# Cross-attention kernel: output tiles of batches 11 to 14 copied by ScalarE with the residual added by GpSimd, and query scores ahead of key scores in the late rounds

## The reference

```python
text = encoder_hidden_states[:, :end_pos]          # 248 of 256 keys
ip_h = encoder_hidden_states[:, end_pos:]          # the last 8
q = _split_heads(hidden_states @ w_q, HEADS)
k = _split_heads(text @ w_k, HEADS)
v = _split_heads(text @ w_v, HEADS)
out_text = _merge_heads(_sdpa(q, k, v))
k_ip = _split_heads(ip_h @ w_k_ip, HEADS)
v_ip = _split_heads(ip_h @ w_v_ip, HEADS)
out_ip = _merge_heads(_sdpa(q, k_ip, v_ip, mask=mask_ip))
out = out_text + IP_SCALE * out_ip
out = out @ w_out + b_out
out = out + residual
```

## Time and profile before

| | us |
|---|---|
| median of three executions | 508.52 |
| lowest and highest | 507.38, 508.76 |
| the profiled execution's own time | 508.77 |
| its span | 506.9 |
| round 12 | 419.45 to 440.35 |
| round 13 | 440.35 to 460.38 |
| round 14 | 460.38 to 480.42 |
| rounds 15 and 16 | 480.42 to 506.9 |

### The profile page before, as it was taken

How to read it: one execution, slowest core, us unless ns; L and a number is a source line. 1 busy time by engine, 2 the same in 40 slices (tenths; PEclk the granted TensorE clock), 3 DMA queues, 4 the chain that set the end, 5 groups by cost and what they waited for, 6 DMA issues and landing times.

```text
span 506.9 us, 11023 instructions
## 1 busy us (share of the span) xinstructions
PE 465.9 (92%) x4250; PEld 319.7 (63%) x4250; DVE 391.2 (77%) x705; ACT 275.3 (54%) x357; POOL 154.1 (30%) x242
## 2 busy tenths in 40 slices
PE   2899486999999999999999999999999998889987
PEld 2698364676666766676667766676667765555543
DVE  3824484796978789697978789697978788999933
ACT  3733022565646476456645566556645555666672
POOL 4490010313304152313204142323204141533442
PEclk9989695999999999999999999999999999999999
DMA  8989996929486585929495675939495655483021
GB/s 270 292 219 232 328 290 188 318 66 306 135 257 205 148 259 162 328 75 319 132 276 185 188 239 151 328 79 308 131 283 180 194 181 156 156 263 87 7 58 53
DMA packets 96453, 101.80 MB, mean 201 GB/s; under 512 B 16896, under 2 KB 83504, under 8 KB 96400
## 3 DMA queue, kind: packets, MB, share of 16 engines
q1 hardware_dynamic: 95408, 98.92, 63.1%
q0 software_dynamic: 992, 2.17, 2.0%
HBM read 67.87 MB, written 33.23 MB: 199 GB/s over the span
## 4 chain that ended last, share of the span: by engine, by line
PE 66%; DVE 14%; issue 7%; DMA 7%; ACT 3%; SPq 2%; POOL 1%; POOLq 0%; ACTq 0%
PE pv L819 15%; PE pj L828 10%; PE score_t L804 10%; PE score_q L743 6%; DVE max_cols L595 5%; PE score_q L694 4%; PE score_q L689 3%; PE score_q L695 3%; PE score_q L691 3%; PE score_q L696 3%; PE score_q L690 3%; PE score_q L698 2%; DVE qk_out L587 2%; PE score_q L699 2%; DMA v_rows<-v_out 1%
## 5 line engine op out<-in xcount | busy, mean ns | idle before, releaser
L520 ACT ACTIVATE probs<-score_t 128x1024 f32<-128x1024 f32 x155 | 158.3, 1021 | 139.5 <-PE score_t L804 139.2
L595 DVE TENSOR_REDUCE max_cols<-score_q 128x4 fp32r<-128x992 f32 x155 | 183.1, 1181 | 65.4 <-PE score_q L743 64.8
L819 PE MATMUL pv<-probs,v_cur 128*32 128x256 f32 x1920 | 120.2, 383 | 2.2 <-ACT probs L520 2.1
L434 POOL TENSOR_TENSOR o_turned<-o_turned,inv_cols 128x256 f32<-128x256 f32 x80 | 53.9, 674 | 158.0 <-DVE inv_cols L645 157.9
L819 PEld LDWEIGHTS pv<-probs,v_cur 128*32 128x32 f32 x1920 | 54.6, 109 | 40.6 <-issue 3.2
L426 POOL TENSOR_TENSOR x_all<-x_all,bias_sb 128x640 f32<-128x640 f32 x16 | 25.0, 1564 | 137.6 <-DMA x_all<-in_x 137.6
L828 PE MATMUL pj<-wo_sb,o_all 128*128 128x320 f32 x186 | 63.2, 460 | 4.0 <-DVE o_all L650 3.9
L512 ACT ACTIVATE o_all<-pv 128x512 f32<-128x512 f32 x80 | 47.8, 598 | 30.0 <-PE pv L819 29.3
L642 DVE STREAM_TRANSPOSE o_turned<-o_all 128x512 f32<-128x512 f32 x80 | 55.5, 693 | 10.9 <-ACT o_all L512 10.9
L804 PE MATMUL score_t<-q_stack,k_stack 64*128 64x256 f32 x420 | 52.9, 330 | 7.3 <-ACT probs L520 5.9
L804 PEld LDWEIGHTS score_t<-q_stack,k_stack 64*128 64x128 f32 x420 | 31.6, 186 | 44.3 <-issue 35.7
(11 more groups left out here) (163 smaller groups left out, 683.3 us busy)
## 6 DMA issues: line engine op xcount, KB each, us to landing
k_stack<-k_parts SPq DMA_DIRECT2D x33, 320.0 KB, 5.0
q_stack<-q_parts SPq DMA_DIRECT2D x33, 320.0 KB, 5.5
q_parts<-qk_out SPq DMA_DIRECT2D x32, 256.0 KB, 4.7
k_parts<-qk_out SPq DMA_DIRECT2D x32, 248.0 KB, 5.2
raw<-in_ctxT SPq DMA_DIRECT2D x14, 512.0 KB, 4.5
v_rows<-v_out SPq DMA_DIRECT2D x32, 160.0 KB, 5.0
v_stage<-v_rows SPq DMA_DIRECT2D x16, 320.0 KB, 6.2
x_all<-in_x SPq DMA_DIRECT2D x16, 320.0 KB, 6.1
```

Source lines behind the costliest of these rows:

```text
L434: pool.tensor_tensor(out, out, inv_cols[:, n % SLOTS, :].unsqueeze(2).broadcast_to([P, 2 * S // 32, DH]), ALU.mult).then_inc(scaled, 1)
L520: nc.scalar.activation(probs[:, slot(t % 2, p), :], key_bank(t, p), ACT.Exp, scale=SCALE)\
L595: nc.vector.tensor_reduce(out=max_cols[:, h, :, at:at + 4:2].rearrange("p t e -> p e t"), in_=both[:, :, :, 0:TEXT], op=ALU.max, axis=AX.X ...
L819: last = mm(pv[32 * t:32 * t + 32, at:at + S], values_of(u, kind, 4 * k + t), probs[:, slot(u, 2 * k + t // 2), a:a + S], start=kind != 1, ...
```

## The change

Three things change. For batches 11 to 14 (`copied`), ScalarE copies the output tile from PSUM to `out_sb` (`copy_out`, same p and same round as `finish` had), signals `out_evac`, and GpSimd adds the residual in place (`add_residual`), which counts `out_done` in the place of VectorE's add. TensorE then waits for `out_evac` and not for `out_done` before it overwrites `pj`. GpSimd adds tile 0 of batch b-1 in `normalise(b)` behind the third quad, and tile 1 of batch b-2 at the head of `normalise(b)`, ahead of the bias; the two of batch 14 come in `normalise(15)` and after it. In rounds above 11, TensorE makes the query scores of a pair ahead of its key scores. SyncE's program is the same. Batches up to 10 and batch 15 are finished by VectorE as before.

```diff
+        def copied(b):
+            return LAST_HOST <= b < B - 1
+        def out_added(eng, b, tiles):
+            n = OT * b + tiles
+            if copied(b) and tiles:
+                eng.wait_ge(out_evac, n - OT * LAST_HOST)
+            elif tiles or not copied(b - 1):
+                need(eng, out_done, n)
+            else:
+                eng.wait_ge(out_evac, n - OT * LAST_HOST)
...
+            def add_residual(b, t):
+                pool.wait_ge(out_evac, OT * (b - LAST_HOST) + t + 1)
+                pool.wait_ge(biased, b + 1)
+                pool.tensor_tensor(out_sb[:, t, :], out_sb[:, t, :], x_res[:, b % 2, t, :], ALU.add).then_inc(out_done, 1)
             def normalise(b):
                 u = b % 2
+                if copied(b - 2):
+                    add_residual(b - 2, 1)
                 pool.wait_ge(xr_loaded[u], 8 * (b - u) + 16)
...
+                    if k == 2 and copied(b - 1):
+                        add_residual(b - 1, 0)
             spread_values(0)
             pool.wait_ge(ld["small"], 32)
             for b in range(B):
                 normalise(b)
+            add_residual(B - 2, 1)
...
+            def copy_out(b, t):
+                act.wait_ge(out_ready, OT * b + t + 1)
+                if t == 0:
+                    act.wait_ge(out_stored, 16 * b)
+                nc.scalar.activation(out_sb[:, t, :], out_bank(b, t), ACT.Copy).then_inc(out_evac, 1)
...
+                    for m, off in FINISH.get(p, ()):
+                        if there(t + off) and copied(t + off):
+                            copy_out(t + off, m)
...
                     for m, off in FINISH.get(p, ()):
-                        if there(t + off):
+                        if there(t + off) and not copied(t + off):
                             finish(t + off, m)
...
                 if c == 0:
-                    need(pe, out_done, OT * b + (t if b < B - 1 else 0))
+                    out_added(pe, b, t if b < B - 1 else 0)
...
                 for p in range(PAIRS):
+                    if there(t + 1) and t > LAST_HOST:
+                        query_scores(t + 1, p)
                     if there(t):
                         key_scores(t, p)
-                    if there(t + 1):
+                    if there(t + 1) and t <= LAST_HOST:
                         query_scores(t + 1, p)
```

More of the change, by code:

```diff
@@ L171, in xattn @@
         o_ready = sem("o_ready")
+        out_evac = sem("out_evac")
         out_ready, out_done, out_stored = sem("out_ready"), sem("out_done"), sem("out_stored")
```

## The result

| | before | with the change |
|---|---|---|
| median of five executions, us | 507.93 | 511.67 |
| lowest and highest | 506.55, 508.76 | 509.70, 512.84 |
| the profiled execution, and its span | 508.77, 506.9 | 511.26, 509.4 |

The ratio is 1.0073 with a 95% interval of 1.0043 to 1.0103: the change makes the kernel slower, by 2.2 to 5.2 us. The two profiled executions differ by 2.5 us, and their traces show where.

The account below looks back on a forecast made before the run. The late rounds were taken to be bound by a loop of TensorE and ScalarE, not by VectorE. Terms -0.4 + 0.04 + 0.35 + 0.9 + 2.0 = +2.9, added to the median 508.52, gave 511.4 us; range 508.8 to 513.0.

Parts of the forecast that it names:

- the opening: Round 12 up to quad 2's values: second key group queued behind the wait for VectorE's last host tile, +0.9 us.
- the end: VectorE's first batch 15 add waits until batch 14's store, behind GpSimd's last add, has landed: +2.0 us.
- the middle: From batch 12's quad 2 values to batch 14's quad 4 values; holds the -0.4 and the two +0.02 terms.
- VectorE's adds: Residual adds taken off VectorE, 0.35 us each; none on the path of rounds 13 and 14, counted 0.
- Query scores first: Rounds 12 to 14: 0.08 us gained at each of five TensorE stands without a copy, -0.4 us.
- The copies at p = 0: Rounds 13 and 14: ScalarE's copy between evacuation and odd exponential, mostly paid for by the new order, +0.02 us each.
- The copies at p = 7: ScalarE's copy fills an idle stretch of 0.60 us between two exponentials, counted 0.
- The copy in round 15: No query scores make room there, so ScalarE's copy delays the exponential TensorE waits for: +0.35 us.
- GpSimd's adds: A 320-column add takes 0.8 us; SyncE's later stores and loads in rounds 13 to 15 counted 0.

Follow-up runs that it names:

- double adds: Kernel before, with each VectorE residual add of batches 11 to 14 preceded by the same add to an unread place; ratio 1.0017.
- short exponentials: Kernel before, with odd-pair exponentials of rounds 12 to 14 covering 768 of 1024 columns; middle 46.73 against 48.21 us, one execution of 508.66 us.
- the kernel with the order only: Kernel before plus only query scores first above round 11; no ScalarE copies or GpSimd adds, VectorE finishes all tiles; ratio 1.0007.
- two of the variants: Kernel before with only the copies and GpSimd adds, ratio 1.0072; the change with pair 1 of round 12 in the old order, ratio 1.0046.
- a buffer of its own: The whole change, but VectorE's last two adds (batch 15) write to a separate buffer; ratio 1.0032.
- the add ahead: The whole change, with ScalarE's last copy ahead of the last evacuation and GpSimd's last add ahead of the last quad; ratio 1.0039.
- the three variants with +0.8 us: The whole change with batch 14 finished by VectorE, a separate buffer for batch 15, or the last add ahead; ratios 1.0051, 1.0032, 1.0039.
- copies-only kernel: Kernel before plus only ScalarE's copies and GpSimd's adds, TensorE still making key scores first; ratio 1.0072.

## Why the prediction was right

**The sum.** Forecast +2.9 on the span, measured +2.5; forecast 511.4, measured 511.67, within the range. The four stretches of the trace give +2.54. On the span the forecast was 0.35 too high, by the terms below: 0.2 in the opening and 0.3 in the end too much, 0.2 in the middle too little. That the time still comes out 0.3 above the forecast is partly luck: against 507.93, the median of the five executions before, the change costs 3.7 us, and the traces explain 2.5 of them.

**VectorE's adds, 0.** Right, and the strongest point of the argument: double adds cost 0.16, short exponentials give 1.48.

**Query scores first, -0.4.** 0.08 for each stand was right where no copy is in the way (0.075, seven times). But the working put 0.34 between key scores and values, and the rows after have 0.43 (432.79 to 433.22). Key scores that have no other scores right in front of them and none behind them cost that much. The same 0.43 stands in the kernel before, in round 15, where key scores have no query scores either (480.42 to 480.85). The error was hidden at the stands without a copy, since another one of the same size stood against it: from the odd key scores to the exponential I had taken 0.55, and behind query scores it is 0.45 (434.99 to 435.44).

**The copies at p = 0, +0.02 each.** This is the step that was mis-sized. There the evacuation and the copy set the exponential, the 0.45 doesn't help, and the 0.43 counts in full. From the values before it to those of quad 0, the change takes 3.90 us (441.53 to 445.43), before 3.80 (441.02 to 444.82): +0.10 each. With that the middle should be -0.2, and it is -0.18. So what was to show in rounds 13 and 14, 0.1 to 0.2 less than 20.03, came out smaller: from the first scores of each round to those of the next they take 19.99 and 19.96. The copies at p = 7 cost nothing, as forecast: without a copy on its path a stand takes 3.72 or 3.73 from values to values, in the change as in the kernel with the order only.

**The copy in round 15, +0.35.** Measured +0.32, evacuation to exponential 0.81 against 0.50. In the five kernels without it the stretch is 16.91 or 16.92, in the six with it 17.24 or 17.25.

**The opening, +0.9.** Measured +0.68. That the wait for `lo_done` would come in front of the second key scores was right: without that, 0.55 goes. The values of quad 0 were 1.5 late, counted from the start of the round, and not 1.7, since the swap of the first pair delayed the end of that wait by 0.14 and not by 0.34: ScalarE's exponential came 0.23 later (the 0.45 again), and VectorE, which before went straight from its maxima to the host tile, lost only a part of that. The part given back was right: 7.77 for the stretch that was forecast as 7.85 - 0.08.

**GpSimd's adds.** 0.8 was forecast for one, 0.86 to 0.87 measured, all eight of them. 320 columns more, the bias add of 640, cost 0.70 on top of 0.86, so about 0.16 depends on no columns, an estimate from these two rows. The proportional estimate from the Trainium skill's GPSIMD Engine Reference (section "Elementwise — side-by-side cycle accounting"), 0.7, is too low here by that much. That SyncE's later stores would hurt nobody was right: the middle of the changed kernel has no wait for a DMA. The waits in two of the variants stand at the first key scores of round 13, ahead of the first store that waits for a GpSimd add, batch 11's in the same round.

**The end, +2.0.** Measured +1.72, in its place and by its mechanism: five kernels take the wait away in three ways (VectorE finishes batch 14, a buffer of its own, the add ahead), and the end is 6.34 to 6.36 in each. The landing was sized by a row of 2.6 us of the kernel before, and took 2.3.

**What stays open.** By their traces, the three variants with +0.8 us should be slower by 0.16%. Their executions say 0.32 to 0.51%; one of the three intervals leaves 0.16% out, one begins at it, one holds it. The copies-only kernel and the double adds show about 0.7 us more by the middle of their intervals than by the trace, the change 1.2 us. The programs are the same up to round 12, and yet in the profiled executions round 12 starts anywhere from 418.7 to 421.5, which is more than what is missing. Only one execution of each kernel has a trace, so whether the surplus lies ahead of round 12 or in late rounds that went otherwise in other executions is open. The stretches are what the argument rests on.

## What to carry to other kernels

When a residual add is handed from one engine to another, follow the tile to its last user: where a buffer is used again right away, its next writer waits for the new engine's add and then for the store's landing of 2.3 us. The place in the queue decided here, not the engine: with the last add one quad earlier the end was that of before. And before work is taken off the busiest engine, look at what ends the stands of the one that waits; 94% busy with no stand to its name was worth 0, and 63% busy at the end of every stand was worth its full time.

## What the runs showed that was not expected

The cost of a group of matmuls depends on what stands beside it. Four key-score matmuls that follow query scores without a gap reach ScalarE's exponential 0.45 us after their start; those that follow anything else, 0.54 to 0.55. It makes no difference whether a stand is in front of them (before, 455.80 to 456.35) or the projection without a gap, as in round 15 of the kernel before (TensorE's key scores and values, ScalarE's exponential):

```profile
480.42 0.50 PE L804 MATMUL score_t<-q_stack,k_stack 64*128 64x256 f32 x4
480.85 1.50 PE L819 MATMUL pv<-probs,v_cur 128*32 128x256 f32 x24
...
480.96 1.02 ACT L520 ACTIVATE probs<-score_t 128x1024 f32<-128x1024 f32 x1 [1.38 <-PE score_t L804]
```

The values too start 0.43 behind such a group, and 0.33 behind one that follows other scores without a gap. The granted clock of round 13 is 1.00 in both kernels, and so it is here, so it is not the clock. What in TensorE makes the difference no run shows.

The rows of maxima for a batch's first key scores travel by two DMAs, and how early they arrive varies from one execution to the next by more than a microsecond. The change had 3.55 us between the issue of the load and the key scores, the kernel before 2.69, and two variants 2.22, where the key scores stood for them.
